# A stack of eight blocks in one kernel: zero rows, plane loads, and shared experts beside a front, reordered

## The chip, the cores and the metric

The kernel runs on one core of one Trainium2 chip. The metric is the device time of one execution in microseconds. All arithmetic here is f32, apart from some bf16 tables of ones and zeros.

## The reference, cut to what matters

The input is 4096 tokens of 256 values. Eight blocks are added to it one after another:

```python
x = x + _L0_attn_a_ref(_layernorm(x), ...)   # mamba: conv, scan over 4 x 1024 steps, 512 channels, 16 states
x = x + _L0_ffn_ref(_layernorm(x), ...)      # 8 experts, top 2, capacity-limited
x = x + _L0_attn_b_ref(_layernorm(x), ...)   # RWKV
x = x + _L0_ffn_ref(_layernorm(x), ...)
x = x + _L1_attn_a_ref(_layernorm(x), ...)   # ssm scan, 256 channels, 16 states; 4 experts, top 2; rms norm with norm_w
x = x + _L1_ffn_ref(_layernorm(x), ...)
x = x + _L1_attn_b_ref(_layernorm(x), ...)   # attention, 16 heads
x = x + _L1_ffn_ref(_layernorm(x), ...)

# _L1_ffn_ref, used twice:
shared = silu(xf @ Sg) * (xf @ Su) @ Sd      # for every token
topk_p, topk_i = top_k(softmax(xf @ Wr), 2)  # 16 experts
y = silu(xf @ wg) * (xf @ wu) @ wd           # each expert, summed with its weights c
return routed + shared
```

## The kernel before, in words

The tokens stand in SBUF as `residual` (`K.X`), 32 tiles of 128 tokens, worked on in eight chunks of four tiles (512 tokens). Stages follow each other. Each engine (V is DVE, S is ACT, G is POOL, T is PE, Q is SP) has its own order of instructions, written out by hand; events (semaphores) tie them together. Each of SP's transfers is issued in the order written, and a wait there holds what stands behind it.

**Scans.** `Scan` (lines 272 on) runs mamba and ssm: a unit is one state of one chunk. SP broadcasts the unit's rows of B and C to all partitions (512 KB, `s_bc`, line 350), into a ring of six buffers. POOL multiplies (line 434), three units ahead; ACT makes the decays, DVE scans, PE sums. `Scan.program` also runs sides beside the units, cut into pieces by ticks: `front(c)` makes the inputs of a chunk, `early(c)` adds up its incoming residual. In the prologue `front(0)` and `early(1)` advance tick by tick together. In the mamba scan SP puts one zero transfer behind every fourth unit (`sync_zero_rows`, line 98): five of 1032 KB to the rows sorted by expert, then eight of 1024 KB to the two planes of results, which later experts fill by token.

**Planes.** A token has two expert results, one in each plane of `results_by_token`. `Planes.sync_tile` (line 1021) loads one tile of both planes, 128 KB each, so eight transfers per chunk. RWKV, the ssm stage and the first stage of sixteen experts take their incoming results so. In the ssm stage `PairSum` has ACT make diagonal matrices of the weights (line 1089), PE multiply by them (line 1100) and DVE add to the residual (line 2473); normalisation on ACT (line 2551) and PE's transposes (line 2656) follow.

**The ssm route.** After the scan a route picks two of four experts for each token, and `SlotTable` makes the list of rows to gather, in eight groups: DVE compares (lines 953, 956), ACT (965) and POOL (975) multiply, PE sums (984). `R.vector_tiles` (lines 881 to 893) finds the expert of each tile and the final weights; `table.vector_rows` (991 to 1000) makes the row numbers. `fold` multiplies the down weights by the inner gain on DVE (line 2737). PE waits for it ahead of the first expert tile; POOL's gathers (line 2281) wait for the row numbers.

**Sixteen experts with a shared expert** (`moe1_stage`, twice). The first use begins with what the ssm block owes: `NormedCombine` adds the two planes (DVE, line 1130), squares (ACT, 1140), takes a root (POOL, 1146), scales and adds to the residual (DVE, 1158, 1162). Then normalise (ACT, 2873), transpose (PE, 2942), copy (ACT, 2890), logits (PE, 2948). This is the front of a chunk. After all eight fronts the shared expert runs chunk by chunk on PE: gate and up (line 2959), down (line 2969). Beside it DVE routes and makes the slot table. For the first three chunks (`BESIDE`), during which DVE routes, POOL does the products and the additions to the residual from ACT's copies; later DVE does them. The slot table's groups stand two by two ahead of chunks 3 to 6 on DVE, the tile steps and row numbers ahead of chunk 7. The planes of a chunk are loaded into the buffers of the shared expert's activations, which are free in the front. SP's order there: planes of chunks 0 and 1, router and shared weights, 32 expert weights (line 2824), then planes of chunk 2 and a row store.

## Time and profile before

| what | us |
|---|---|
| median of 3 runs | 5258.45 |
| lowest, highest | 5258.2, 5264.23 |
| profiled execution | 5258.9 |
| its span | 5257.2 |
| PE, DVE, POOL, ACT busy | 4016.0, 2871.3, 2504.2, 2291.7 |
| mamba scan | to about 1040 |
| 8 experts, RWKV, 8 experts | to 2364 |
| ssm scan; route and four-expert tiles | to 2946; to 3400 |
| front of 16 experts; shared expert; expert tiles | to 3521; to 3630; to 3780 |
| attention; second stage of 16 experts with the end | to 4851; to 5257 |

The profile is of one execution, and its stages follow each other on one core, so a share of busy time over the whole span is a mean over stages with different limits. Each place of the change is to be read in its own stage: what ended the last wait there.

### The profile page before, as it was taken

Reading aid. Unit: us, or ns where it says so; the run is one execution under the profiler, and the core shown is the slowest. Engines: PE = TensorE matmul, PEld = TensorE weight load, DVE = VectorE, ACT = ScalarE, POOL = GpSimd, SP = SyncE. Lnnn points to the kernel's source line nnn. Section 1 sums busy time; section 2 is a strip of 40 time slices with the busy share of each in tenths; the row PEclk is TensorE's granted clock in tenths of the full one; section 3 lists DMA queues with packets and bytes.
Section 4 is the critical chain, followed back from the end, with each engine's and each line's share of the span. In section 5 each row is a group of like instructions: output and inputs, shape, how many; then the busy total and the mean of one; then the engine's idle time right before and its main releaser. Section 6 shows DMA issues by size and latency. Waiting matters only on the chain.

```text
span 5257.2 us, 49460 instructions
## 1 busy us (share of the span) xinstructions
PE 4016.0 (76%) x14864; PEld 2274.2 (43%) x14866; DVE 2871.3 (55%) x5621; ACT 2291.7 (44%) x4134; POOL 2504.2 (48%) x2152
## 2 busy tenths in 40 slices
PE   5788888769948778995777699849757677777892
PEld 2333333357715556772333366536522222223671
DVE  5899999841156663115888622264344545455432
ACT  5565666321156663114555233333335444555341
POOL 4899999822222333115778444324542413122355
PEclk8999999969968888997888799959857777788796
DMA  7765555512110001214555311231552222220245
GB/s 154 188 158 140 136 143 145 144 49 101 63 49 23 26 25 59 101 58 132 153 148 144 98 45 46 62 122 52 145 95 39 51 39 44 37 37 20 68 126 131
DMA packets 326109, 472.75 MB, mean 90 GB/s; under 512 B 36458, under 2 KB 182870, under 8 KB 325770
## 3 DMA queue, kind: packets, MB, share of 16 engines
q1 hardware_dynamic: 292416, 389.08, 28.2%
q0 software_dynamic: 29184, 76.12, 5.2%
...
## 4 chain that ended last, share of the span: by engine, by line
PE 36%; DVE 8%; ACT 6%; issue 5%; POOL 5%; DMA 3%; SPq 1%; DVEq 0%; POOLq 0%; ACTq 0%
PE s_gate_up L2303 7%; PE s_result_sum L2319 4%; PE s_hidden_sum L1742 3%; PE s_result_sum L1753 3%; PE s_out_sum L3603 3%; PE s_scores_T L3590 2%; PE s_shared L2959 2%; PE s_scores L3554 2%; DVE s_decay L369 2%; ACT s_weights_T L3409 1%; PE s_shared L2969 1%; POOL s_gathered L1043 1%; POOL s_h L434 1%; PE s_transposed L2293 1%; PE s_mid_transposed L2312 1%
## 5 line engine op out<-in xcount | busy, mean ns | idle before, releaser
L434 POOL TENSOR_TENSOR s_h<-s_dtu,s_bc 128x1024 f32<-128x1024 f32 x384 | 902.7, 2362 | 121.8 <-PE s_y_sum L476 77.8
L476 PE MATMUL s_y_sum<-s_h,identity 128*128 128x512 f32 x1536 | 791.0, 655 | 160.4 <-POOL s_h L443 146.2
L401 ACT ACTIVATE s_decay<-s_dt,s_A 128x512 f32<-128x512 f32 x768 | 498.4, 681 | 339.7 <-DVE s_h L376 333.2
L476 PEld LDWEIGHTS s_y_sum<-s_h,identity 128*128 128x128 f32 x1536 | 302.4, 207 | 611.6 <-issue 321.7
L3409 ACT ACTIVATE s_weights_T<-s_scores_T 128x1024 f32<-128x1024 f32 (+3 forms) x384 | 300.3, 812 | 403.7 <-PE s_scores_T L3590 402.3
L2303 PE MATMUL s_gate_up<-s_w_gate_up,s_rowsT 128*128 x1184 | 419.2, 486 | 2.6 <-issue 2.1
L3473 POOL TENSOR_SCALAR_AFFINE_SELECT s_weights_T<-s_weights_T 128x256 f32<-128x256 f32 x256 | 104.3, 411 | 625.1 <-ACT s_weights_T L3409 623.1
L443 POOL TENSOR_TENSOR s_h<-s_h,s_bc 128x512 f32<-128x512 f32 x256 | 326.3, 1275 | 43.6 <-DVE s_h L369 26.5
L2362 DVE TENSOR_TENSOR s_mid<-s_act,s_gate_up 128x128 f32<-128x128 f32 (+1 forms) x228 | 92.7, 407 | 454.8 <-ACT s_act L2335 454.8
L369 DVE TENSOR_TENSOR_SCAN s_decay<-s_decay,s_h 128x512 f32<-128x512 f32 x256 | 307.6, 1217 | 53.4 <-POOL s_h L434 26.3
L369 DVE TENSOR_TENSOR_SCAN s_decay<-s_decay,s_carry,s_h 128x512 f32<-128x512 f32 x256 | 322.4, 1275 | 23.7 <-ACT s_decay L401 10.3
L376 DVE TENSOR_TENSOR s_h<-s_decay,s_bc 128x512 f32<-128x512 f32 x512 | 331.1, 666 | 0.0
L2281 POOL DMA_INDIRECT s_rows<-rows_by_token,s_rows_at x228 | 235.4, 1032 | 163.4 <-issue 92.7
...
L1742 PE MATMUL s_hidden_sum<-s_rowsT,s_w_inter 128*128 128x320 f32 x1024 | 282.0, 437 | 0.9 <-ACT s_rowsT L1677 0.9
L1753 PE MATMUL s_result_sum<-s_w_exp_out,s_hidden 128*128 128x256 f32 x1280 | 279.1, 379 | 1.1 <-issue 1.1
L3554 PE MATMUL s_scores<-s_keys,s_queries 96*128 96x512 bf16 (+3 forms) x550 | 194.3, 393 | 101.0 <-DVE s_maxima L3254 27.9
L3251 DVE CUSTOM_DVE_ANT_0 s_scores<-s_scores,s_mask_add 128x256 f32<-128x256 f32 (+2 forms) x380 | 189.2, 509 | 134.3 <-PE s_scores L3554 125.1
L2303 PEld LDWEIGHTS s_gate_up<-s_w_gate_up,s_rowsT 128*128 128x128 f32 x1184 | 209.6, 192 | 116.0 <-issue 105.6
L1686 ACT ACTIVATE s_hidden<-s_hidden_sum 128x320 f32<-128x320 f32 x128 | 56.0, 437 | 467.3 <-PE s_hidden_sum L1742 467.3
L3590 PE MATMUL s_scores_T<-s_queries,s_keys 99*128 99x512 bf16 (+3 forms) x768 | 218.0, 373 | 53.1 <-DMA s_queries<-parts_of_max 32.8
L1753 PEld LDWEIGHTS s_result_sum<-s_w_exp_out,s_hidden 128*128 128x128 f32 x1280 | 241.9, 190 | 34.3 <-issue 2.1
...
## 6 DMA issues: line engine op xcount, KB each, us to landing
s_bc<-s_bc_rows SPq DMA_DIRECT2D x384, 512.0 KB, 5.4
sorted_results<-s_result SPq DMA_DIRECT2D x160, 128.0 KB, 2.3
s_w_inter<-in_L_ffn_experts_inter SPq DMA_DIRECT2D x16, 1024.0 KB, 5.1
s_w_exp_out<-in_L_ffn_experts_out SPq DMA_DIRECT2D x16, 1024.0 KB, 8.2
...
results_by_token<-zeros SPq DMA_DIRECT2D x8, 1024.0 KB, 8.0
...
```

The source lines that it names most:

```text
L369: V.e.tensor_tensor_scan(decay if d < k else self.h[r][:, d, :], decay, self.h[r][:, d, :], self.carry[:, i, d:d + 1] if c % CPB else 0.0, ...
L376: V.e.tensor_tensor(self.h[r][:, d, :], self.decay[:, (2 * g + d) % 4, :], self.bc[r][:, 1, :], ALU.mult).then_inc(*(self.weighed_v if d = ...
L401: S.e.activation(self.decay[:, (2 * g + d) % 4, :], dt[q // self.passes % 2][:, at, :], ACT.Exp, scale=A[:, at, g % ns:g % ns + 1]).then_i ...
L434: G.e.tensor_tensor(self.h[r][:], dtu[q // self.passes % 2][:, at:at + 2, :], mid(self.bc[r][:, 0, :], 2), ALU.mult).then_inc(*self.fed.up())
L443: G.e.tensor_tensor(h, h, self.bc[g % self.RING][:, 1, :], ALU.mult).then_inc(*self.weighed_g.up())
L476: made = T.e.matmul(self.y[:, d, :], ident[:], self.h[r][:, d, :], start=False, stop=g % ns == ns - 1)
L1742: made = T.e.matmul(hb[half][:, 0:HALF], w_in[r][:, k, i * P:(i + 1) * P], xsT[r][:, k, half * HALF:(half + 1) * HALF], start=k == 0, stop ...
L1753: made = T.e.matmul(ob[n % 2][:, 0:D], hT[:, i, t * P:(t + 1) * P], w_out[r][:, i, :], start=i == 0, stop=i == KI - 1)
L2303: made = T.e.matmul(self.gb[j % 2][:, at:at + n], self.xT[j % 2][:, k, :], self.gu_flat[:, bass.ds(expert[j] * (DT * 2 * F) + (k * 2 * F + ...
L3409: S.e.activation(PT[n % 2][:, 2 * pair:2 * pair + 2, o:CH], st[pair][:, :, o:CH], ACT.Exp, scale=HD ** -0.5).then_inc(*weighed.up())
L3554: T.e.matmul(f[:, 0:n_keys], QS[u % 2][0:ROWS, h, qt * P:(qt + 1) * P], KS[u % 2][0:ROWS, h, half * CH:half * CH + n_keys], start=True, st ...
L3590: made = T.e.matmul(st[pair][:, i, o:CH], KS[u % 2][:, h, kt * P:(kt + 1) * P], QS[u % 2][:, h, qh * CH + o:(qh + 1) * CH], start=True, st ...
```

## The change

Five parts. (1) The zeros go out in transfers of half the size, planes first, one behind every eighth unit. (2) The planes of a chunk come in two transfers of 512 KB. (3) In the ssm prologue `early(1)` runs 24 ticks behind `front(0)`. (4) In the ssm route the fold goes from DVE to ACT, and the tile steps go behind the row numbers. (5) In the first stage of sixteen experts three chunks of the shared expert stand in the front, two beside the route, and the slot table comes after chunk 4; SP issues four weights per chunk behind that chunk's planes.

```diff
@@ sync_zero_rows
-        for to, n, half in ((self.sorted_in, CAPPED_SLOTS // P, D // 2 + 1), (self.planes, 2 * NT, D // 2)):
-            for s0 in range(0, n, 8):
-                Q.e.dma_start(to[s0 * P:(s0 + 8) * P, :].rearrange("(p a) (b c) -> p (a b) c", p=P, b=2),
-                              mid(self.zeros[:, 0:half], 16)).then_inc(*self.zeroed.dma())
+        for to, n, width in ((self.planes, 2 * NT, D), (self.sorted_in, CAPPED_SLOTS // P, D + 2)):
+            for s0 in range(0, n, 4):
+                Q.e.dma_start(to[s0 * P:(s0 + 4) * P, :].rearrange("(p a) c -> p a c", p=P),
+                              mid(self.zeros[:, 0:width], 4)).then_inc(*self.zeroed.dma())
@@ Scan.program
-            second.until(tick)
+            second.until(tick - self.behind)
@@ mamba_stage
-        sc.sync(rows_made, rows[32:64, :], lambda g: steps(zeros, 1 if g % 4 == 3 else 0))
+        sc.sync(rows_made, rows[32:64, :], lambda g: steps(zeros, 1 if g % 8 == 7 else 0))
@@ Planes
+    def sync_half(self, c, i):
+        self.K.Q.e.dma_start(self.to(c)[i], self.from_dram[i][:, chunk_tiles(c), :]).then_inc(*self.arrived[c % 2].dma())
+    def sync(self, c):
+        self.sync_half(c, 0)
+        self.sync_half(c, 1)
@@ ssm stage
-    sc = Scan(K, M, 1, NS, (1, 2), prologue=32)
+    sc = Scan(K, M, 1, NS, (1, 2), prologue=32, behind=24)
-            c, i = divmod(g, NS)
-            if c + 3 < NC and i % 2 == 0 and i < 2 * TPC:
-                pieces(c + 3, range(i // 2, i // 2 + 1))
+            c, n = divmod(g, NS)
+            if c + 3 < NC and n in (2, 6):
+                pairs.sync_half(c + 3, n // 4)
...
     def fold():
-        V.wait_ge(*weights_here.now())
-        flat = w_d[:].rearrange("p e k c -> p (e k) c")
-        V.e.tensor_tensor(flat, flat, last(gain[:].rearrange("p e k -> p (e k)"), D), ALU.mult).then_inc(*folded.up())
+        S.wait_ge(*weights_here.now())
+        for e in range(E):
+            for k in range(F // P):
+                made = S.e.activation(w_d[:, e, k, :], w_d[:, e, k, :], ACT.Copy, scale=gain[:, e, k:k + 1])
+        made.then_inc(*folded.up())
...
-        if g == 2:
-            R.vector_tiles()
     table.vector_rows()
-    fold()
+    R.vector_tiles()
@@ moe1_stage
-    BESIDE = 3
+    early = K.owed == "normed"
+    BESIDE, EARLY = (5, 3) if early else (3, 0)
-        owed = NormedCombine(K, MS, xn, norm_w, hs + hm)
-    copies = MS.sb("shared_copies", [P, 2, CH])
+        owed = NormedCombine(K, MS, xn, norm_w, [R.work[:, 2 * i:2 * i + 2, :] for i in range(4)])
+    copies = [MS.sb(f"shared_copies{i}", [P, 2, CH]) for i in range(2 if early else 1)]
+    FRONTS = in_order("f0 f1 f2 f3 f4 f5 f6 f7")
+    ORDER = in_order("f0 f1 i0 f2 f3 o0 i1 f4 f5 o1 i2 f6 f7 o2") if early else FRONTS
+    GPSIMD_ORDER = in_order("f0 f1 f2 f3 i0 f4 f5 o0 i1 f6 f7 o1 i2 o2") if early else FRONTS
...
         for c in range(NC):
             if owed is not None and c + 2 < NC:
                 owed.sync_chunk(c + 2)
+            for e in range(c * E // NC, (c + 1) * E // NC):
+                for j, n in enumerate(("Wg", "Wu")):
+                    Q.e.dma_start(w_gu[:, e, :, j * F:(j + 1) * F],
+                                  W["L1_ffn_" + n][e].rearrange("(k p) f -> p k f", p=P)).then_inc(*experts_here.dma())
             Q.wait_ge(*ln.used.at(c))
...
+        for kind, c in ORDER:
+            {"f": front, "i": shared_in, "o": shared_out}[kind](c)
+        for c in range(EARLY, max(NC, LAST)):
+            if c < NC:
+                shared_in(c)
+                shared_out(c)
+            if c == EARLY:
+                R.tensor_rank()
             for g in groups(c):
                 table.tensor_group(g)
```

`f` is a front, `i` the gate and up part of a shared chunk (`shared_in`), `o` its down part (`shared_out`); ACT and PE follow `ORDER`, POOL `GPSIMD_ORDER`. DVE keeps its fronts, route, groups in that order; with `LAST` now 9, its groups stand ahead of chunks 5, 6, 7 and behind chunk 7.

On PE, in the ssm prologue (`s_pair_0`, `s_pair_1` are a chunk's planes), before, from the middle of chunk 1's eight pair products, behind which chunk 0's transposes stand:

```order
L1100 MATMUL s_front<-s_pair_0,s_pair_weights 128x256
L1100 MATMUL s_front<-s_pair_1,s_pair_weights 128x256
L2656 MATMUL s_front<-identity,s_xn 128x128 x8
L2662 MATMUL s_front<-s_xT,s_w_bc 32x512 x2
L2670 MATMUL s_front<-s_xT,s_w_delta 128x512 x2
L2671 MATMUL s_front<-s_ones_row,s_b_delta 128x512
L2670 MATMUL s_front<-s_xT,s_w_delta 128x512 x2
L2671 MATMUL s_front<-s_ones_row,s_b_delta 128x512
L2678 MATMUL s_front<-identity,s_stat 1x128 x3
```

and now, from chunk 0's last two products:

```order
L1104 MATMUL s_front<-s_pair_0,s_pair_weights 128x256
L1104 MATMUL s_front<-s_pair_1,s_pair_weights 128x256
L2657 MATMUL s_front<-identity,s_xn 128x128 x8
L2663 MATMUL s_front<-s_xT,s_w_bc 32x512 x2
L2671 MATMUL s_front<-s_xT,s_w_delta 128x512 x2
L2672 MATMUL s_front<-s_ones_row,s_b_delta 128x512
L2671 MATMUL s_front<-s_xT,s_w_delta 128x512 x2
L2672 MATMUL s_front<-s_ones_row,s_b_delta 128x512
L2679 MATMUL s_front<-identity,s_stat 1x128 x3
L1104 MATMUL s_front<-s_pair_0,s_pair_weights 128x256
L1104 MATMUL s_front<-s_pair_1,s_pair_weights 128x256
```

The transposes (line 2657 now) stand directly behind chunk 0's eight products; chunk 1's stand behind the bound's products (line 2679).

On PE, in the first stage of sixteen experts, before (the last two fronts, then the shared chunks):

```order
L2942 MATMUL s_shared<-identity,s_y_rows 128x128 x8
L2948 MATMUL s_logits<-s_w_router,s_xT 128x16 x8
L2942 MATMUL s_shared<-identity,s_y_rows 128x128 x8
L2948 MATMUL s_logits<-s_w_router,s_xT 128x16 x8
L2959 MATMUL s_shared<-s_xT,s_w_shared_gate_up 128x512 x8
L2969 MATMUL s_shared<-s_w_shared_down,s_shared_mid 128x256 x8
L820 MATMUL s_rank_within_tile<-s_mask,before 128x512
L820 MATMUL s_tile_totals<-s_mask,ones_bf 128x512
L2959 MATMUL s_shared<-s_xT,s_w_shared_gate_up 128x512 x8
L2969 MATMUL s_shared<-s_w_shared_down,s_shared_mid 128x256 x8
L2959 MATMUL s_shared<-s_xT,s_w_shared_gate_up 128x512 x8
L2969 MATMUL s_shared<-s_w_shared_down,s_shared_mid 128x256 x8
```

and now, from the first front on:

```order
L2975 MATMUL s_shared<-identity,s_y_rows 128x128 x8
L2981 MATMUL s_logits<-s_w_router,s_xT 128x16 x8
L2975 MATMUL s_shared<-identity,s_y_rows 128x128 x8
L2981 MATMUL s_logits<-s_w_router,s_xT 128x16 x8
L2991 MATMUL s_shared<-s_xT,s_w_shared_gate_up 128x512 x8
L2975 MATMUL s_shared<-identity,s_y_rows 128x128 x8
L2981 MATMUL s_logits<-s_w_router,s_xT 128x16 x8
L2975 MATMUL s_shared<-identity,s_y_rows 128x128 x8
L2981 MATMUL s_logits<-s_w_router,s_xT 128x16 x8
L3003 MATMUL s_shared<-s_w_shared_down,s_shared_mid 128x256 x8
L2991 MATMUL s_shared<-s_xT,s_w_shared_gate_up 128x512 x8
L2975 MATMUL s_shared<-identity,s_y_rows 128x128 x8
```

A gate and up piece (line 2991) stands behind each pair of fronts, a down piece (line 3003) behind the next pair.

On DVE, at the end of the ssm route, before (tile steps between the third and fourth group):

```order
L881 TENSOR_TENSOR s_tile_compare<-iota,s_end_tile 128x320
L882 TENSOR_REDUCE s_tile_expert_f<-s_tile_compare 128x80
L883 TENSOR_SCALAR s_tile_expert_f<-s_tile_expert_f 128x80
L884 CAST s_tile_expert<-s_tile_expert_f 128x80
L886 CAST pick_row<-s_slots 128x32 x2
L889 TENSOR_TENSOR s_route_red<-pick_weight 128x32
L890 TENSOR_SCALAR s_route_red<-s_route_red 128x32
L891 RECIPROCAL s_route_red<-s_route_red 128x32
L893 TENSOR_TENSOR pick_weight<-pick_weight,s_route_red 128x32 x2
L894 ISA
L953 TENSOR_TENSOR s_one_hots<-iota,s_tile_of 128x640
```

and now, behind the last group:

```order
L957 TENSOR_TENSOR s_one_hots<-iota,s_lane_of 128x1024
L992 TENSOR_SCALAR s_row_of_place<-s_result_sum 128x80
L997 TENSOR_TENSOR s_row_of_place<-s_row_of_place,s_result_sum 128x80
L1006 TENSOR_SCALAR s_empty_place<-s_row_of_place 128x80
L1008 SCALAR_TENSOR_TENSOR s_results_at<-s_row_of_place,s_empty_place 128x80
L1001 TENSOR_SCALAR s_rows_at<-s_results_at 128x80
L882 TENSOR_TENSOR s_tile_compare<-iota,s_end_tile 128x320
L883 TENSOR_REDUCE s_tile_expert_f<-s_tile_compare 128x80
L884 TENSOR_SCALAR s_tile_expert_f<-s_tile_expert_f 128x80
L885 CAST s_tile_expert<-s_tile_expert_f 128x80
```

The tile steps (line 882 on) stand behind the row numbers (line 1001), and no fold follows on DVE.

## Rows read from the trace of the kernel before

**Rows 1.** Windows of the mamba scan: busy time of POOL's products (line 434).

```profile
core 0: us, POOL busy (x), PEclk, DMA share, GB/s
51.00:160.00 109.00, 51.75 (x23) 0.79 0.90 166
160.00:280.00 120.00, 71.29 (x31) 0.92 0.76 201
280.00:960.00 680.00, 435.37 (x186) 0.93 0.55 143
```

**Rows 2.** DMA issues between 50 and 160 us: KB each, median us to landing.

```profile
s_bc<-s_bc_rows SPq DMA_DIRECT2D x23, 512.0 KB, 10.4
sorted_rows<-zeros SPq DMA_DIRECT2D x5, 1032.0 KB, 14.9
results_by_token<-zeros SPq DMA_DIRECT2D x1, 1024.0 KB, 7.7
```

**Rows 3.** Waits between 51 and 160 us: us in total, times, longest.

```profile
POOL s_h L434 <- DMA s_bc<-s_bc_rows: 20.1, 5, 7.1
```

**Rows 4.** Timeline at the start of the ssm stage: start, us, engine, line.

```profile
2374.67 0.23 ACT L2538 ACTIVATE s_A<-s_A 128x32 f32<-128x32 f32 x1 [31.76 <-DMA s_norm_w<-in_L_norm_w]
...
2389.93 2.07 ACT L2551 ACTIVATE s_xn<-residual,s_rn_addend,s_rn_factor 128x256 f32<-128x256 f32 x4 [12.11 <-POOL s_rn_addend L243]
...
2399.65 1.22 DVE L2473 TENSOR_TENSOR residual<-residual,s_front 128x1024 f32<-128x1024 f32 x1 [11.88 <-PE s_front L1100]
2400.91 1.40 DVE L220 BATCH_NORM_STATS2 s_rn_stats<-residual 128x6 f32<-128x256 f32 x4
...
2401.02 1.06 PE L2656 MATMUL s_front<-identity,s_xn 128*128 128x128 f32 x8 [1.41 <-DVE residual L2473]
```

**Rows 5.** Timeline of the ssm route and its first gather.

```profile
2967.52 1.54 DVE L881 TENSOR_TENSOR s_tile_compare<-iota,s_end_tile 128x320 bf16<-128x320 f32 x1
...
2971.88 0.83 DVE L953 TENSOR_TENSOR s_one_hots<-iota,s_tile_of 128x640 bf16<-128x640 f32 x1
...
2984.46 0.83 ACT L965 ACTIVATE s_one_hots<-s_one_hots,s_own_lane 128x640 bf16<-128x640 bf16 x1 [2.10 <-DVE s_one_hots L953]
...
2989.14 0.20 DVE L1000 TENSOR_SCALAR s_rows_at<-s_results_at 128x80 int32<-128x80 int32 x1
2989.26 4.42 DVE L2737 TENSOR_TENSOR s_w_down<-s_w_down,s_inner_gain 128x4096 f32<-128x4096 f32 x1
2990.23 4.51 POOL L2281 DMA_INDIRECT s_rows<-rows_by_token,s_rows_at  x1 [3.56 <-DVE s_rows_at L1000]
...
2996.74 0.66 PE L2293 MATMUL s_transposed<-identity,s_rows 128*128 128x128 f32 x2 [8.70 <-DMA s_rows<-rows_by_token,s_rows_at]
```

**Rows 6.** Window of the first front of sixteen experts, all engines.

```profile
3400.00:3520.00 120.00, 41.55 (x185) 38.38 (x186) 64.25 (x176) 41.76 (x113) 25.13 (x41) 0.50 0.54 164
```

**Rows 7.** SP's queue in that front: the second sixteen weight transfers.

```profile
3420.21 8.15 SPq L2824 DMA_DIRECT2D s_w_gate_up<-in_L_ffn_Wu  x16
```

**Rows 8.** DVE's timeline in that front: the wait for chunk 2's planes.

```profile
3442.43 3.38 DVE L1130 SCALAR_TENSOR_TENSOR s_y_rows<-s_shared_act,pick_weight,s_y_rows 128x256 f32<-128x256 f32 x8 [19.45 <-DMA s_shared_act<-results_by_token]
```

**Rows 9.** PE's timeline from that front to the end of the shared expert.

```profile
3463.92 3.60 PE L2948 MATMUL s_logits<-s_w_router,s_xT 128*128 128x16 f32 x16 [2.18 <-ACT s_xT L2890]
...
3505.40 3.60 PE L2948 MATMUL s_logits<-s_w_router,s_xT 128*128 128x16 f32 x16 [3.13 <-ACT s_xT L2890]
...
3518.07 3.59 PE L2948 MATMUL s_logits<-s_w_router,s_xT 128*128 128x16 f32 x16 [0.69 <-ACT s_xT L2890]
3521.51 9.97 PE L2959 MATMUL s_shared<-s_xT,s_w_shared_gate_up 128*128 128x512 f32 x16
...
3539.47 7.03 PE L2959 MATMUL s_shared<-s_xT,s_w_shared_gate_up 128*128 128x512 f32 x16
...
3566.63 7.03 PE L2959 MATMUL s_shared<-s_xT,s_w_shared_gate_up 128*128 128x512 f32 x16
...
3617.18 7.07 PE L2959 MATMUL s_shared<-s_xT,s_w_shared_gate_up 128*128 128x512 f32 x16
3625.20 3.69 PE L2969 MATMUL s_shared<-s_w_shared_down,s_shared_mid 128*128 128x256 f32 x16 [0.94 <-DVE s_shared_mid L2861]
```

109 lines of the change are left out of this document (57 added, 52 removed).

## The prediction, made before the result was known

> **What bounds the kernel now.** I read the page first, then the stages as windows, then in each stage the waits, and last the timelines around every wait that the change touches. One engine after another sets the pace on this core, so the change is costed stage by stage: mamba scan, RWKV start, ssm start, ssm route, first front of the sixteen experts with its shared expert.
>
> In the mamba scan POOL's products run back to back once the zeros are stored: 680 us for 186 units, 3.66 us each, at a DMA share of 0.55. While the zeros go out, 23 units take 109 us at a share of 0.90 and 31 take 120 at 0.76 [rows 1]. At 3.66 a unit these 54 would take 197.6, so 31.4 us are lost: 24.8 in the first window and 6.6 in the second. The reader is to see that POOL waits for the broadcast of B and C itself, 20.1 us in five waits, which the later windows don't have [rows 3], and that a zero transfer of sorted rows (pieces of 516 B) lands after 14.9 us while one of the result planes (pieces of 512 B) takes 7.7, and that a broadcast beside them takes 10.4 [rows 2].
>
> At the start of the ssm stage PE's transposes of chunk 0 start at 2401.02, though their input is ready at 2392.00 (2389.93 + 2.07): in PE's order the pair sum of chunk 1 stands before them, and its bank is free only when DVE has added it [rows 4]. In the ssm route the chain ends in DVE's table rows, then the first gather, whose issue takes 4.51 us beside DVE's 4.42 us fold, and PE starts at 2996.74 [rows 5].
>
> In the front of the sixteen experts PE is at 1.2 GHz for all 120 us and busy for a third of them [rows 6]. DVE stands 19.45 us for a pair of planes that is queued on SP behind 32 weight transfers, the last 16 of which take 8.15 us to issue [rows 7, 8]. Then comes the shared expert, a PE chain of eight chunks that ends the stage [rows 9].
>
> **The zeros.** Bytes and SP issues: 13 transfers become 26 of half the size, spread over 207 units in place of 51. From the shares, one broadcast costs 0.55 x 3.66 = 2.0 us of all DMA engines. The first window holds 0.90 x 109 - 23 x 2.0 = 52 us of zeros, five of sorted rows and one of planes; the second 0.76 x 120 - 31 x 2.0 = 29 us for seven of planes, so 4.1 each, and 9.6 each for sorted rows. Halved blocks: 2.1 and 4.8 us, now one per 29 us. The DMA engines are then never full. The lowest loss is nothing. The highest that the nearest rows give is by size: a plane block of 4.1 us lost 0.9 each (6.6 over seven), so sixteen at 0.5 and ten sorted blocks at 1.1 lose 19. I take the middle, **10, so 21 us gained** (bounds 12 and 31), since the ring holds three units of lead against a block shorter than one and a half. Pieces of 1,032 B may be cheaper than 516 B ones; no row shows a size above 512 B with an odd end, and I give nothing for it. The Trainium skill ("DMA: Bandwidth & Descriptors", Specifications) says that pieces of 512 B or more run at line rate, by which 516 B pieces should cost what 512 B pieces do; by that rule the halving saves only queueing. The rows above disagree with it, by more than twofold.
>
> **The planes in two transfers per chunk in place of eight.** SP issues six fewer, some 0.46 us each. Bytes are the same. At the RWKV start the first pair comes up to 2.7 us earlier, of which I take 1; at the first front 0.5; elsewhere other work hides them.
>
> **ssm start.** Constants follow the first pair on SP, and ACT waits for the last of them until 2374.67 [rows 4]: 2.3 earlier. Transposes of chunk 0 can follow their normalisation: 9.0 earlier. Against it: PE comes to them colder (I take 3.5, bounds 0 and 9, the length of the doubled PE work); DVE's add and statistics of chunk 1 (1.22 + 1.40 + 0.38 = 3.0) now stand in scan unit 1, where DVE is near its limit; 1.0 for ACT's weights and POOL's factors there. Sum **+4** (bounds -2 and +8).
>
> **ssm route.** The tile steps of 4.36 us (2967.52 to 2971.88) leave the chain and stand behind the row numbers. The row numbers are then ready at 2985.0. The fold leaves DVE; sixteen ACT steps of 128x256, 0.52 us each by the four normalising steps of that size (2.07 [rows 4]), take 8.3 us from 2980.9 on (2984.46 + 0.83 less 4.36 [rows 5]), so end at 2989.2, before the first gathered rows. The first gather needs 1.0 to issue in place of 4.51 and some 2 to land: PE starts near 2990.2 in place of 2996.74: **+6.5** (bounds 3, if the moved tile steps now lengthen the gather as the fold did, and 7.9, both terms in full).
>
> **First front with three shared chunks inside.** SP now issues pairs ahead of weights, so 16 of the 19.45 us go and the logits of chunk 1 end at 3451.3, not 3467.5 (3463.92 + 3.60 [rows 9]). Then PE runs shared-in of chunk 0, 9.97 at the low clock as measured, to 3461.3. Two rounds follow of two fronts, an out and an in. Two fronts took 20.7 where a transfer held them (3463.92 to 3505.40, halved) and 12.7 at the end (3505.40 to 3518.07). Now ACT serves both fronts and shared work in strict order, so I take 20.3. Out plus in takes 10.7 at full clock (7.07 + 3.69 less overlap [rows 9]), 21.3 at half; I take 14.1 as the clock climbs. Two rounds are 68.8, the last two fronts 12.7 and 1.6 for ACT's turn: logits end at 3544.4, **22.7 later** than 3521.66. Behind them stand one out and five chunks: 5.4 for the out with its wait, 27.2 for the two chunks beside the route (3539.47 to 3566.63), 3 x 12.6 (3566.63 to 3617.18 is four), 2 for DVE's last add: 72.4, where from 3521.7 to that add before (3625.20 + 3.69 + 0.7) it was 107.9. Then what used to be covered: groups 6 and 7 of the slot table with the row numbers, 6.9 (five took 17.3, from 2971.88 to 2989.14 [rows 5]), and the tile steps, 4.4, less some 2 in which they fill DVE's idle time: 9.3; and 0.9 from the row numbers to the gather (2989.34 to 2990.23 [rows 5]). First gather at 3627.0; before, by the same 0.9 behind the last add, at 3630.5. Of these 3.5 I take **+2.5**, one off for the loads on POOL and ACT that no row shows beside the new order (bounds -17, everything shared at the low clock, and +28). What was 108 us of well packed PE is now packed into a front that has other limits, so most of what leaves the tail returns in the front.
>
> The second such stage keeps its order; its SP order changes, but nothing waits there for pairs: nothing.
>
> **Sum.** 21 + 1 + 4 + 6.5 + 0.5 + 2.5 = 35.5 us off the profiled execution's 5258.9, 5223.4. The median of the runs is 5258.45, so the two stand 0.45 apart, which I leave alone.
>
> **Rivals.**
> 1. *Fast front.* DVE's chain lets the fronts run at 12.7 a pair, and shared work lifts PE to 2.4 GHz early: 2 x 7.6 + 2 x 3.4 + 3 for the first shared-in at full clock = 25 more: 5198. For it: the tail of the front before did 12.7. Against: ACT's order couples fronts to PE's shared results.
> 2. *Low clock.* Each shared piece stands between waits and stays at 1.2 GHz, as PE did all through this front [rows 6]: 14 for two rounds, 5 for the first chunks behind: 5242. The Trainium skill ("TensorE: Matmul & The Clock Gate", HAM oscillation) describes bursts between waits that start cold each time. By that rule the trace agrees: 0.50 for 120 us [rows 6], and the first shared-in takes 9.97 against 7.07 later.
> 3. *Zeros still cost.* The upper loss of 19: 5232.
> 4. *Zeros don't gain.* If transfer time alone counted, all 81 us of it stay and the loss stays 31.4: 5244. That is the skill's rule above taken at its word.
> 5. *Slower.* On the queue each zero block stands between two broadcasts. If a broadcast is held for the block's whole time and POOL with it, 16 x 2.1 + 10 x 4.8 = 82 us are lost in place of 31.4: 5295. It makes the kernel slower once more than 56 of the 82 are exposed (31.4 + 14.5 of other gains + 10.5). Before, 31.4 of 81 were, with full engines. Unlikely.
>
> **Chances.** Forecast 0.45, rival 1 0.18, rival 2 0.15, rival 3 0.12, rival 4 0.03, rival 5 0.04, something else 0.03. The range goes from rival 1 to rivals 2 and 4, 5198 to 5244. This kernel can be told from no change at 0.2%, 10.5 us. Only rivals 2 to 4 together come within that (0.06); slower 0.04; faster 0.90.
>
> **What would show it.** Right: in the mamba scan no long POOL wait for a broadcast, and units 23 to 54 at 3.7 us; PE's transposes of chunk 0 right behind ACT's normalisation; a first ssm gather of 1.0 us; no 19 us DVE stall, the last logits some 22 us later, the first gather of the sixteen experts about 2 to 3 us earlier. Wrong: a granted clock of 0.50 through the interleaved front, POOL waits at every eighth scan unit, or DVE as the last to end before the first gather by more than 10 us.

## The result, and the profile after

The changed kernel takes 5221.05 us (median of 4 runs, 5211.93 to 5230.75), the kernel before 5258.32 (4 runs, 5254.15 to 5264.23). The ratio is 0.9929, 95% interval 0.9908 to 0.9949. The forecast was 5223, so the total came as forecast, to within 2 us. The terms behind it did not all do so, and that is what the rest is about.

The profiled execution of the changed kernel is the longest of its four: 5230.75 us, span 5229.0, against a span of 5257.2 before. Cut at the first instruction of each stage in the two traces (SP's first transfer, or PE's first expert product; the front of sixteen experts is cut from its rest at DVE's first step of the route, and the rest ends at POOL's first gather), the 28.2 us between the spans fall like this. The medians lie 37.3 us apart, so the table accounts for an execution that gained less than the median one.

| stretch, from first instruction to first instruction | before | changed | difference | forecast |
|---|---|---|---|---|
| mamba scan | 1038.82 | 1004.33 | -34.5 | -21 |
| 8 experts, to RWKV | 406.95 | 406.93 | 0.0 | 0 |
| RWKV | 600.20 | 607.53 | +7.3 | -1 |
| 8 experts | 319.00 | 320.39 | +1.4 | 0 |
| ssm stage | 582.14 | 583.95 | +1.8 | -4 |
| route, to the first expert product | 49.63 | 43.59 | -6.0 | -6.5 |
| four-expert tiles | 405.59 | 406.69 | +1.1 | 0 |
| front of 16 experts | 119.37 | 135.64 | +16.3 | +22.2 |
| rest of that stage, to the first gather | 108.83 | 83.97 | -24.9 | -25.2 |
| expert tiles | 145.10 | 146.44 | +1.3 | 0 |
| attention | 1077.13 | 1085.49 | +8.4 | 0 |
| second stage of 16 experts, end | 404.44 | 404.05 | -0.4 | 0 |

**Scan.** POOL's products in the changed kernel in the windows of [rows 1] (columns as there):

```profile
51.00:160.00 109.00, 67.55 (x29) 0.84 0.58 157
160.00:280.00 120.00, 75.11 (x33) 0.92 0.60 158
280.00:960.00 680.00, 440.97 (x188) 0.94 0.60 160
```

62 units by 280 us where there were 54, and in these windows the DMA share is never above 0.60. The issues while the planes' zeros go out (60 to 520 us), and then the sorted rows' (520 to 820 us), to be read beside [rows 2]:

```profile
results_by_token<-zeros SPq DMA_DIRECT2D x16, 512.0 KB, 5.8
```

```profile
s_bc<-s_bc_rows SPq DMA_DIRECT2D x82, 512.0 KB, 4.8
sorted_rows<-zeros SPq DMA_DIRECT2D x10, 516.0 KB, 7.2
```

A broadcast lands after 4.8 us here, and after 4.7 in the window of [rows 2], where it took 10.4 before; a half block of sorted rows lands after 7.2. From 51 us to the end of the scan POOL waited 29.6 us in ten waits for broadcasts in the kernel before ([rows 3] has five of them). In the changed kernel it waits 0.2 us, once.

**ssm start.** PE's timeline, to be read beside [rows 4]:

```profile
2364.10 1.97 PE L2657 MATMUL s_front<-identity,s_xn 128*128 128x128 f32 x8 [7.46 <-ACT s_xn L2552]
...
2371.47 3.78 PE L2671 MATMUL s_front<-s_xT,s_w_delta 128*128 128x512 f32 x4 [0.68 <-ACT s_rows L2568]
...
2377.18 3.78 PE L2671 MATMUL s_front<-s_xT,s_w_delta 128*128 128x512 f32 x4
```

The transposes stand 0.06 us behind the normalisation, as forecast, but each group of delta products takes 3.78 us, where the kernel before took 1.98. The window of all engines (busy of PE, its weight loads, DVE, ACT and POOL, then the granted clock, DMA share and GB/s) has the clock beside it, 0.50, the lower of PE's two levels (1.2 of 2.4 GHz), though PE is busy 10.96 of these 12 us:

```profile
2372.00:2384.00 12.00, 10.96 (x12) 2.84 (x10) 0.13 (x1) 1.00 (x1) 0.00 (x0) 0.50 0.53 137
```

Then, from the timeline of all engines:

```profile
2401.33 0.36 SPq L1022 DMA_DIRECT2D s_pair<-results_by_token  x1
...
2401.73 9.89 SPq L351 DMA_DIRECT2D s_bc<-s_bc_rows  x4
...
2407.60 2.35 POOL L435 TENSOR_TENSOR s_h<-s_dtu,s_bc 128x1024 f32<-128x1024 f32 x1 [4.27 <-DMA s_bc<-s_bc_rows]
```

SP's first load of chunk 3's planes waits there until PE has summed the pair of chunk 1; broadcasts stand behind it and POOL waits 4.27 us.

**Route.** The rows that answer to [rows 5]:

```profile
2961.85 0.20 DVE L1001 TENSOR_SCALAR s_rows_at<-s_results_at 128x80 int32<-128x80 int32 x1
2961.97 0.48 DVE L882 TENSOR_TENSOR s_tile_compare<-iota,s_end_tile 128x320 bf16<-128x320 f32 x1
...
2962.94 1.20 POOL L2283 DMA_INDIRECT s_rows<-rows_by_token,s_rows_at  x1 [3.56 <-DVE s_rows_at L1001]
...
2966.72 0.66 PE L2295 MATMUL s_transposed<-identity,s_rows 128*128 128x128 f32 x2 [5.97 <-DMA s_rows<-rows_by_token,s_rows_at]
```

The compare of the tile steps takes 0.48 us where it took 1.54 beside a POOL product. The gather is issued in 1.20 us, not 4.51.

**Front of sixteen experts.** DVE's timeline, the stalls only, then PE's, to be read beside [rows 8] and [rows 9], and windows of the front and of the rest (columns as in [rows 6]):

```profile
3405.27 3.38 DVE L1133 SCALAR_TENSOR_TENSOR s_y_rows<-s_route_work,pick_weight,s_y_rows 128x256 f32<-128x256 f32 x8 [4.13 <-DMA s_route_work<-results_by_token]
...
3435.00 0.17 DVE L1158 TENSOR_SCALAR s_y_sums<-s_y_sums 128x4 f32<-128x4 f32 x1 [13.37 <-ACT s_y_squares L1143]
...
3466.71 0.17 DVE L1158 TENSOR_SCALAR s_y_sums<-s_y_sums 128x4 f32<-128x4 f32 x1 [14.55 <-ACT s_y_squares L1143]
...
3509.05 0.69 DVE L836 TENSOR_REDUCE s_route_red<-s_logits 128x32 f32<-128x512 f32 x1 [26.50 <-PE s_logits L2981]
```

```profile
3419.20 3.60 PE L2981 MATMUL s_logits<-s_w_router,s_xT 128*128 128x16 f32 x16 [7.59 <-ACT s_xT L2902]
3422.63 9.69 PE L2991 MATMUL s_shared<-s_xT,s_w_shared_gate_up 128*128 128x512 f32 x16
...
3451.85 5.31 PE L3003 MATMUL s_shared<-s_w_shared_down,s_shared_mid 128*128 128x256 f32 x16
3457.00 7.03 PE L2991 MATMUL s_shared<-s_xT,s_w_shared_gate_up 128*128 128x512 f32 x16
...
3484.51 6.04 PE L3003 MATMUL s_shared<-s_w_shared_down,s_shared_mid 128*128 128x256 f32 x16
3490.39 7.03 PE L2991 MATMUL s_shared<-s_xT,s_w_shared_gate_up 128*128 128x512 f32 x16
...
3505.41 3.59 PE L2981 MATMUL s_logits<-s_w_router,s_xT 128*128 128x16 f32 x16 [0.69 <-ACT s_xT L2902]
...
3514.51 7.03 PE L2991 MATMUL s_shared<-s_xT,s_w_shared_gate_up 128*128 128x512 f32 x16
```

```profile
3373.41:3509.05 135.64, 73.03 (x273) 55.14 (x274) 64.42 (x177) 50.97 (x129) 37.42 (x50) 0.64 0.49 145
3509.05:3593.02 83.97, 65.97 (x241) 40.41 (x242) 61.63 (x77) 20.03 (x30) 30.78 (x18) 0.91 0.01 2
```

The 19.45 us stall is gone, but DVE now stands 13.37 and 14.55 us for squares, which ACT takes behind its turn with a shared chunk.

### The profile page after: what moved, and what is told of

Read it like the earlier page. It is cut to its first block, busy times and chain, and to the rows that moved or that the text cites. A ratio compares the mean times of both kernels' runs of the same rounds, so it can differ in the third digit from the quotient of the medians.

```text
span 5229.0 us, 49359 instructions
## 1 busy us (share of the span) xinstructions
PE 4032.2 (77%) x14864; PEld 2280.5 (44%) x14866; DVE 2867.2 (55%) x5612; ACT 2302.5 (44%) x4158; POOL 2513.9 (48%) x2160
## 4 chain that ended last, share of the span: by engine, by line
PE 38%; DVE 8%; ACT 6%; issue 4%; POOL 4%; DMA 3%; SPq 1%; DVEq 0%; POOLq 0%; another core or an unknown queue 0%; ACTq 0%
PE s_gate_up L2305 7%; PE s_result_sum L2321 4%; PE s_hidden_sum L1745 3%; PE s_result_sum L1756 3%; PE s_out_sum L3641 3%; PE s_scores_T L3628 2%; PE s_shared L2991 2%; PE s_scores L3592 2%; DVE s_decay L370 2%; PE s_shared L3003 1%; ACT s_weights_T L3447 1%; POOL s_gathered L1047 1%; POOL s_h L435 1%; PE s_transposed L2295 1%; DVE s_maxima L3292 1%
## 5 line engine op out<-in xcount | busy, mean ns | idle before, releaser
L477 PE MATMUL s_y_sum<-s_h,identity 128*128 128x512 f32 x1536 | 774.2, 644 | 124.4 <-POOL s_h L444 112.8
L3628 PE MATMUL s_scores_T<-s_queries,s_keys 99*128 99x512 bf16 (+3 forms) x768 | 220.7, 378 | 45.2 <-DMA s_queries<-parts_of_max 33.9
```

What stands on the lines that cost most here:

```text
L477: made = T.e.matmul(self.y[:, d, :], ident[:], self.h[r][:, d, :], start=False, stop=g % ns == ns - 1)
L3628: made = T.e.matmul(st[pair][:, i, o:CH], KS[u % 2][:, h, kt * P:(kt + 1) * P], QS[u % 2][:, h, qh * CH + o:(qh + 1) * CH], start=True, st ...
```

## The experiments

Each stage is closed by a barrier, so several edits can be read in one kernel by the lengths of their stages. The kernel before was run beside each group; its median was 5263.78 (13 runs), 5259.46 (19), 5257.67 (7). Lengths in us from the profile of each, with the median time and the ratio to before:

| kernel | median | ratio (95%) | mamba | RWKV | ssm | route | front + rest | attention |
|---|---|---|---|---|---|---|---|---|
| zeros_only | 5228.13 | 0.9941 (0.9923 to 0.996) | 1001.7 | 607.3 | 583.6 | 49.6 | 118.2 + 105.7 | 1073.0 |
| planes_only | 5251.62 | 0.9981 (0.9971 to 0.999) | 1033.1 | 609.8 | 582.6 | 49.5 | 113.7 + 106.5 | 1073.4 |
| pairs_later | 5216.21 | 0.992 (0.9901 to 0.9939) | 1002.3 | 606.1 | 579.5 | 43.9 | 135.6 + 83.9 | 1078.5 |
| behind_0 | 5222.11 | 0.9926 (0.991 to 0.9943) | 1003.2 | 606.3 | 582.9 | 43.8 | 135.4 + 84.0 | 1078.5 |
| sp_order_only | 5209.84 | 0.9904 (0.9887 to 0.9921) | 1002.3 | 603.8 | 584.8 | 43.4 | 101.8 + 106.4 | 1086.2 |
| order_undone | 5227.33 | 0.9931 (0.991 to 0.9953) | 1003.2 | 607.5 | 584.9 | 44.0 | 114.6 + 106.6 | 1083.2 |
| big_blocks_fold | 5256.24 | 0.9988 (0.9977 to 1.0) | 1029.5 | 610.9 | 583.7 | 46.2 | 119.6 + 107.2 | 1077.0 |
| old_pieces_tiles | 5240.59 | 0.9963 (0.9952 to 0.9975) | 1016.9 | 607.1 | 583.5 | 46.8 | 118.2 + 106.7 | 1076.3 |
| planes_ahead | 5200.31 | 0.9893 (0.9877 to 0.991) | 1006.6 | 605.7 | 580.5 | 43.5 | 90.8 + 106.7 | 1077.1 |
| front_freed | 5201.51 | 0.9892 (0.9875 to 0.9908) | 1007.1 | 605.8 | 579.4 | 43.4 | 115.7 + 83.8 | 1082.5 |
| every_4 | 5227.15 | 0.994 (0.9924 to 0.9957) | 1014.7 | 605.8 | 583.8 | 43.5 | 135.3 + 83.9 | 1078.7 |
| before_again | 5245.11 (1 run) | | 1029.3 | 600.8 | 583.6 | 49.5 | 118.6 + 105.7 | 1074.7 |

### The zeros: zeros_only, big_blocks_fold, old_pieces_tiles, every_4

**zeros_only**: the kernel before with `sync_zero_rows` and its `g % 8 == 7` from the change.

> The kernel before with the zeros of the change alone (half the size, planes first, one behind every eighth unit). Theory A (the loss beside the zeros goes whole, and what the changed kernel lost again in RWKV and attention is the scatter of those stages): the end of the mamba scan comes 33 to 36 us before the 1038.8 us of the kernel before, RWKV takes 598 to 608 us without any tie to the scan, and the total is 25 to 38 us shorter than before. Theory B (half of it is given back later, in RWKV and attention, because of the zeros): mamba 34 us earlier, RWKV 607 us and attention 1085 us again, total 15 to 20 us shorter. The forecast's own term was 21 us with bounds of 12 and 31.

Mamba ends at 1001.7. The three profiles with the old zeros end it at 1038.8, 1029.3 and 1033.1; their mean is 1033.7. The eight kernels with the new zeros end it at 1001.7 to 1007.1, 1003.8 in the mean. So the zeros are worth some 30 us (22 to 37 between single profiles): theory A, not the forecast's 21. The cause is in POOL's waits for broadcasts, which sum to 29.6, 26.2 and 27.0 us in the three profiles with the old zeros and to 0.8 us at most in the eight with the new ones. The total agrees: 0.9941 is 31 us off.

**big_blocks_fold**: in the kernel before

```diff
-        sc.sync(rows_made, rows[32:64, :], lambda g: steps(zeros, 1 if g % 4 == 3 else 0))
+        sc.sync(rows_made, rows[32:64, :], lambda g: steps(zeros, 1 if g % 8 == 7 else 0))
     def fold():
-        V.wait_ge(*weights_here.now())
+        S.wait_ge(*weights_here.now())
...
```

and the sixteen ACT steps of the change called behind the scalar groups.

> The kernel before with two edits in two stages. Zeros: the old 13 transfers of 1 MB, but one behind every eighth unit. Theory A (what counts is that blocks stand too close for the DMA engines to catch up): nearly all of the 31 us goes, mamba ends at 1003 to 1010. Theory B (a single 1 MB block outlasts the ring's lead each time): five sorted blocks still cost 3 to 5 us each, mamba ends at 1018 to 1030. Route: the fold on ACT, tile steps left between the groups. Both theories: first gather issued in 1.0 us, 3.5 us less than the 49.6 from the route's first transfer to the first expert product.

**old_pieces_tiles**: half blocks every eighth unit in the old pieces, and the tile steps moved with the fold left on DVE:

```diff
+        for to, n, half in ((self.planes, 2 * NT, D // 2), (self.sorted_in, CAPPED_SLOTS // P, D // 2 + 1)):
+            for s0 in range(0, n, 4):
+                Q.e.dma_start(to[s0 * P:(s0 + 4) * P, :].rearrange("(p a) (b c) -> p (a b) c", p=P, b=2),
+                              mid(self.zeros[:, 0:half], 8)).then_inc(*self.zeroed.dma())
```

> The kernel before with two edits in two stages. Zeros: half-size blocks, planes first, every eighth unit, but in the old pieces of 512 and 516 B. Theory A (rows: 516 B pieces cost 4.8 us of all DMA engines for half a MB, whatever the spacing): sorted blocks land after about 7 us, as those with 1032 B pieces do, mamba ends at 1002 to 1008. Theory B (piece size matters): sorted blocks of 516 B pieces land later than 8 us, and their DMA share is higher than the changed kernel's 0.63. Route: tile steps behind the row numbers, the fold still on DVE, now behind them: the first gather is issued 4.4 us earlier, but PE waits for the fold, so 2 to 3.5 us less than 49.6.

**every_4**: the changed kernel with `g % 4 == 3` again.

> The changed kernel with the same half-size zero blocks one behind every fourth unit, so the spacing alone goes back. Theory A (halving the block and the whole pieces do it, the ring's lead covers any single block): mamba ends within 5 us of 1004. Theory B (what counts is the bytes per unit of time): DMA share near 0.7 while they go out, mamba ends at 1010 to 1020.

Spaced alone, the 1 MB blocks end mamba at 1029.5, within theory B's range, and POOL's own wait for broadcasts from 51 to 520 us reads

```profile
POOL s_h L434 <- DMA s_bc<-s_bc_rows: 7.3, 4, 4.0
```

That is 7.3 us where 26.2 to 29.6 were waited for at the old spacing, so the scan's end does not follow these waits. What else is in it are two waits of DVE (line 579) for PE's sums at the end of a chunk, 7.01 us to 201.18 and 7.60 us to 446.29; the waits of this kind in the eight kernels with the new zeros are 4.8 at most.

Halved, in old pieces, mamba ends at 1016.9. Halved and in whole pieces, at the 1001.7 to 1007.1 above. The half blocks of the planes in pieces of 512 B and then those of the sorted rows in pieces of 516 B land after

```profile
results_by_token<-zeros SPq DMA_DIRECT2D x16, 512.0 KB, 6.0
```

```profile
sorted_rows<-zeros SPq DMA_DIRECT2D x10, 516.0 KB, 9.0
```

The planes' 6.0 us are what pieces of 1024 B take too (5.8 to 6.0 in the nine kernels that have them), but the sorted rows' 9.0 us stand against 7.2 to 7.9 in pieces of 1032 B, with the same bytes. So theory B was right that they land later than 8 us, though not of the DMA share, which is 0.63 from 520 to 820 us as in the changed kernel. But the late blocks did not hold the broadcasts: POOL waits 1.0 us for them in the whole scan. Of the 15 us over zeros_only 13.7 are two waits of DVE for PE:

```profile
664.76 1.23 DVE L579 TENSOR_TENSOR s_u<-s_y_sum,s_z 128x1024 f32<-128x1024 f32 x1 [6.37 <-PE s_y_sum L476]
...
791.10 1.23 DVE L579 TENSOR_TENSOR s_u<-s_y_sum,s_z 128x1024 f32<-128x1024 f32 x1 [7.31 <-PE s_y_sum L476]
```

Ahead of the second one PE stood at the lower clock (columns as in [rows 6]):

```profile
774.00:790.00 16.00, 13.97 (x16) 4.52 (x15) 9.79 (x11) 11.07 (x18) 14.99 (x8) 0.50 0.55 177
```

Whether the pieces had a part in that, one profile can't say.

Whole pieces at the old spacing (every_4) end mamba at 1014.7, within theory B's 1010 to 1020. Here POOL's waits, small and many, account for the 11 us over the 1003.8; those from 51 to 520 us read

```profile
POOL s_h L435 <- DMA s_bc<-s_bc_rows: 11.6, 11, 1.8
```

big_blocks_fold and old_pieces_tiles also split the route. With the fold alone on ACT it takes 46.2 us, 3.4 off the 49.6 of before; with the tile steps alone moved, 46.8, 2.8 off. The fold's rows in big_blocks_fold, from the timeline of all engines:

```profile
2989.76 6.47 ACT L2738 ACTIVATE s_w_down<-s_w_down,s_inner_gain 128x256 f32<-128x256 f32 x16
...
2994.79 1.19 POOL L2281 DMA_INDIRECT s_rows<-rows_by_token,s_rows_at  x1 [3.56 <-DVE s_rows_at L1000]
...
2997.84 0.66 PE L2293 MATMUL s_transposed<-identity,s_rows 128*128 128x128 f32 x2 [5.23 <-DMA s_rows<-rows_by_token,s_rows_at]
```

Sixteen steps take 6.47 us, 0.40 each, and end before the gathered rows have landed. In old_pieces_tiles, where DVE keeps the fold, the first gather passes it and the third does not:

```profile
2974.21 1.20 POOL L2281 DMA_INDIRECT s_rows<-rows_by_token,s_rows_at  x1 [3.56 <-DVE s_rows_at L1000]
...
2976.70 4.42 DVE L2737 TENSOR_TENSOR s_w_down<-s_w_down,s_inner_gain 128x4096 f32<-128x4096 f32 x1
2977.03 4.97 POOL L2281 DMA_INDIRECT s_rows<-rows_by_token,s_rows_at  x1 [0.30 <-issue]
...
2981.23 0.66 PE L2293 MATMUL s_transposed<-identity,s_rows 128*128 128x128 f32 x2 [9.20 <-DVE s_w_down L2737]
```

PE's transposes there wait 9.20 us, to the fold's end.

Of mamba: the spacing alone doesn't give the gain, and with half blocks in whole pieces the spacing is worth some 11 us, all of it in POOL's waits. What the pieces are worth to the scan is not shown, nor what the block's size is worth by itself: the half blocks go out planes first in every kernel that has them, and repeats of one zero order lie up to 5 us apart with the new zeros and 9.5 with the old.

### Planes and later stages: planes_only, before_again

> The kernel before with two plane transfers of 512 KB per chunk in place of eight of 128 KB. Theory A: nothing but the issues of the first pair in each stage moves; RWKV stays within 4 us of its 600.2, the ssm prologue reaches its first row store 2 us earlier, total within 5 us of before. Theory B: the large transfers cost RWKV its 7 us (607 us instead of 600.2), total 5 to 10 us longer.

> The kernel before once more, for a second profile of its stages. Theory A (a stage scatters by some us from one execution to the next, and the first profile of before had a short RWKV): RWKV 604 to 611 us here, mamba ends at 1032 to 1040. Theory B (the shorter scan or the planes lengthen RWKV): RWKV 600 us again.

**planes_only** is the kernel before with two transfers per chunk. It is 10 us faster (0.9981). Some 5 us of that stand in the front of sixteen experts, 113.7 us where five profiles with eight transfers and the old order read 118.2 to 119.6: SP has twelve issues fewer ahead of chunk 2's planes, and DVE waits for planes 36.3 us there in place of 41.9. The forecast gave 0.5 for that. No stage shows the rest. In RWKV its first chunk is 0.7 to 1.1 us shorter, as forecast. But RWKV as a whole is not settled: the two profiles of the kernel before have 600.2 and 600.8, the changed kernel and its eleven relatives 603.8 to 610.9, three of them (zeros_only, big_blocks_fold, old_pieces_tiles) with not one instruction of RWKV changed. So it is not the planes alone. It may be the scatter of single profiles, though the two of one kernel lie only 0.6 apart. Attention is alike: 1073.0 to 1077.1 in the six profiles of kernels built on the one before, 1077.1 to 1086.2 in the eight built on the changed one, where it has the same instructions. Its windows, before and then changed (columns as in [rows 6]), show which engine took longer over them:

```profile
3775.63:4852.76 1077.13, 749.79 (x3732) 283.12 (x3732) 525.73 (x1591) 498.19 (x648) 327.87 (x424) 0.77 0.24 46
```

```profile
3739.46:4824.95 1085.49, 762.42 (x3732) 287.66 (x3732) 530.68 (x1591) 498.81 (x648) 328.44 (x424) 0.76 0.24 46
```

The same 3732 products keep PE busy 12.6 us longer, at a slightly lower mean clock; ACT and POOL take the same time to within 1 us. So the 8.4 us of attention go with PE's clock. In RWKV it is less plain: PE is busy 7.6 us longer in the changed kernel (434.2 for 426.6), but only 2.1 longer in zeros_only, whose RWKV is as long. What sets the clock stays open; no run here isolates it.

### ssm start: pairs_later, behind_0

```diff
-            if c + 3 < NC and n in (2, 6):
-                pairs.sync_half(c + 3, n // 4)
+            if c + 3 < NC and n in (6, 10):
+                pairs.sync_half(c + 3, n // 8)
```

> The changed kernel with the planes of chunk c+3 issued behind scan units 6 and 10 in place of 2 and 6. Theory A: in the changed kernel SP stands at the planes of chunk 3, which wait until PE has added the pair of chunk 1, now 24 ticks later, and the broadcasts of units 3 on are queued behind (POOL waits 4.3 us). Then the time from POOL's first product to the second row store of the ssm scan goes from 43.6 us back to about 39, and the ssm stage is 4 to 5 us shorter. Theory B: the 43.6 us come from DVE's and ACT's work on chunk 1 that now stands in the first units, and the time stays within 1 us.

SP no longer stands there: seven broadcasts go out ahead of the load.

```profile
2368.56 30.76 SPq L351 DMA_DIRECT2D s_bc<-s_bc_rows  x7
2399.36 0.47 SPq L1022 DMA_DIRECT2D s_pair<-results_by_token  x1
```

From POOL's first product to the second row store it is 42.6 us, not 39 (43.6 in the changed kernel): 1.0 of the 4.7 us over the kernel before was SP's wait, the rest stands beside chunk 1's add, statistics and pair products in the first units. (The kernel before has 38.9 us there in the profile of the forecast and 39.8 in before_again, so the excess may be a microsecond less.) So theory B is right of the interval. Yet the stage is 4.5 us shorter, 3.5 of it before the first product, in the same PE work:

```profile
2366.94 3.78 PE L2671 MATMUL s_front<-s_xT,s_w_delta 128*128 128x512 f32 x4 [0.68 <-ACT s_rows L2568]
...
2371.94 1.98 PE L2671 MATMUL s_front<-s_xT,s_w_delta 128*128 128x512 f32 x4
```

The second group of delta products runs at 2.4 GHz there. This is hardly an accident of one execution: pairs_later, planes_ahead and front_freed, which share the edit, have 1.98 us and 579.4 to 580.5 for the stage; the changed kernel, sp_order_only, order_undone and every_4 have 3.78 and 583.8 to 584.9.

> The changed kernel with chunk 1's pair sum back beside chunk 0's front (behind=0). Theory A: the shift by 24 ticks gains 8.5 us to the first row store and gives all back (5.5 us at PE's low clock, 4.7 us behind SP's wait), so the ssm stage without it is 1 to 3 us shorter than the 583.9 us of the changed kernel. Theory B (the forecast): the shift is worth 2 to 4 us, and without it the stage is that much longer.

**behind_0** (`behind=0` in the changed kernel) has 582.9: theory A. The shift alone costs 1.1 us; with the loads put off it gains 3.4.

### Front of sixteen experts: sp_order_only, order_undone, planes_ahead, front_freed

**sp_order_only** sets `early = False` in the changed kernel: engines in the old order, SP in the new one. **order_undone** takes the whole stage from the kernel before, with its planes in two transfers.

> The changed kernel with the first stage of sixteen experts back in the old engine order (all fronts, then eight shared chunks, three beside the route, table early), but with SP's new order (planes ahead of weights). Stage from its first planes to its first gather: 228.2 us before, 219.6 in the changed kernel. Theory A (SP's order and not the three shared chunks in the front carries the gain): the front takes 100 to 105 us (the 19.45 us stall goes), the tail stays at 106 to 109, so 206 to 214 in all, and this kernel beats the changed one by 5 to 13 us. Theory B (the forecast's working, where the fronts are held by transfers and turns either way): the front loses only 5 to 8 of its 119 us, stage 218 to 222.

> The changed kernel with the whole first stage of sixteen experts as before, SP's order too (planes in two transfers). Theory A: it reads like the kernel before with two plane transfers per chunk alone, 220 to 224 us for the stage, so the reorder is worth only 1 to 4 us of the 8.6 between the two profiles. Theory B: 228 us, the reorder is worth 8 us.

```profile
3367.75:3469.51 101.76, 43.24 (x193) 40.07 (x194) 64.26 (x176) 41.77 (x113) 24.90 (x40) 0.50 0.65 194
```

Theory A, clearly: with SP's order alone the front is 101.8 us and the stage 208.2, where three shared chunks inside make it 219.6, and the old order altogether 221.2. SP's order is worth 13.0 us, and the interleaving gives 11.4 of them back. (With SP's order goes the move of the incoming planes to other buffers, `R.work` in the diff; the two were not run apart.) The total follows: 5209.84. The interleaving lengthens the front by 33.9 us and shortens the rest by 22.5. Of the 33.9, 28.0 are DVE's waits for squares, which sum to 30.3 us in the changed kernel's front and to 2.3 in this one.

What DVE still waits for in it are planes, at every second chunk:

```profile
3399.03 3.38 DVE L1133 SCALAR_TENSOR_TENSOR s_y_rows<-s_route_work,pick_weight,s_y_rows 128x256 f32<-128x256 f32 x8 [3.55 <-DMA s_route_work<-results_by_token]
...
3419.01 3.38 DVE L1133 SCALAR_TENSOR_TENSOR s_y_rows<-s_route_work,pick_weight,s_y_rows 128x256 f32<-128x256 f32 x8 [3.58 <-DMA s_route_work<-results_by_token]
...
3438.92 3.38 DVE L1133 SCALAR_TENSOR_TENSOR s_y_rows<-s_route_work,pick_weight,s_y_rows 128x256 f32<-128x256 f32 x8 [3.50 <-DMA s_route_work<-results_by_token]
```

**planes_ahead** takes these away, with the old engine order and pairs_later:

```diff
+        if owed is not None:
+            owed.sync_chunk(2)
         for c in range(NC):
-            if owed is not None and c + 2 < NC:
-                owed.sync_chunk(c + 2)
...
+            if owed is not None and c + 3 < NC:
+                owed.sync_chunk(c + 3)
             Q.wait_ge(*ln.used.at(c))
```

> Meant as the best version: the changed kernel with all fronts ahead of the shared chunks again (as in the run of SP's order alone), the ssm pair loads behind units 6 and 10, and in the first stage of sixteen experts the planes of chunk c+3 issued ahead of the wait for chunk c's normalisation, where they stood behind it. Theory A (three stalls of 3.5 us of DVE at every second chunk are SP standing in that wait): they go, the front falls from 101.8 to 90 to 93 us, the ssm stage from 584.8 to about 580, total 12 to 17 us under SP's order alone, near 5195. Theory B (the planes would come no earlier, since buffers or bandwidth hold them): front stays above 100, total 4 to 5 us under, near 5205.

DVE's waits for planes, then windows of front and rest:

```profile
DVE s_y_rows L1133 <- DMA s_route_work<-results_by_token: 13.6, 1, 13.6
```

```profile
3368.77:3459.55 90.78, 43.25 (x193) 40.07 (x194) 63.98 (x177) 41.41 (x113) 27.40 (x40) 0.50 0.71 217
3459.55:3566.28 106.73, 93.42 (x322) 54.18 (x322) 64.87 (x85) 24.58 (x38) 31.71 (x21) 0.96 0.00 1
```

The front is 90.8 us: of the waits for planes only the stage's first is left. Theory A of the front; the total, 5200.31, is 9.5 under sp_order_only, less than the 12 to 17 expected. Between the two profiles, which lie 18.5 apart, the stage gives 10.7 (208.2 to 197.5) and the ssm stage 4.4. The others are not edited: attention is 9.1 shorter, the mamba scan 4.3 and RWKV 1.9 longer.

**front_freed** keeps the interleaving but lets DVE and POOL run ahead:

```diff
...
+    SCALAR_ORDER = in_order("f0 f1 s4 i0 f2 f3 s6 o0 i1 f4 f5 o1 i2 f6 f7 o2") if early else FRONTS
-    GPSIMD_ORDER = in_order("f0 f1 f2 f3 i0 f4 f5 o0 i1 f6 f7 o1 i2 o2") if early else FRONTS
+    GPSIMD_ORDER = in_order("f0 f1 f2 f3 f4 i0 f5 f6 o0 i1 f7 o1 i2 o2") if early else FRONTS
...
```

(`s4` is the squares of chunk 4; SP as in planes_ahead, in the ssm stage too.)

> The changed kernel (three shared chunks inside the front) with the ssm pair loads behind units 6 and 10, planes of chunk c+3 ahead of the wait, and the squares of chunks 4 and 6 taken by ACT ahead of its shared piece, POOL's root and factors of chunks 4, 6 ahead of its products. Theory A (the front is long because DVE stands 13.4 and 14.6 us for squares behind ACT's shared piece, which waits for PE): the front falls from 135.6 to 112 to 120 us, the stage to 196 to 205. Theory B (each round is held by PE's shared pieces and ACT's turns, and DVE's wait is slack): front stays at 130 to 136.

```profile
3368.67:3484.39 115.72, 70.14 (x273) 52.74 (x274) 65.58 (x176) 50.65 (x129) 39.22 (x50) 0.66 0.56 170
3484.39:3568.16 83.77, 66.01 (x242) 40.47 (x242) 61.43 (x77) 20.04 (x30) 30.95 (x18) 0.91 0.00 1
```

Theory A: 115.7 us for the front, 19.9 less, and 199.5 for the stage. Two edits share this, and DVE's waits part them: those for squares fall by 13.0 us, from 30.3 to 17.3, and those for planes by 4.7, from 18.4 to 13.7. So the waits behind ACT's turn were the greater part of what the interleaving cost, and 17.3 us of them are left. Its total, 5201.51, can't be told from planes_ahead. Both beat the changed kernel by some 20 us.

## Why the prediction was right, and where its parts were not

- **Zeros, 21 forecast, some 30 measured.** The step that failed is the residual of 10 us, taken as the middle between nothing and 19. With blocks halved, spaced and in whole pieces POOL's wait for broadcasts is 0.2 us: the loss doesn't shrink with the block's size, it ends. The lower bound, nothing, was right. The upper one was no bound: by the forecast's own rows the first window lost 24.8 us to five sorted blocks and one of planes, 4.8 a sorted block where the forecast took 2.2. The forecast also said that later windows have no wait for broadcasts; from 160 to 280 us there were five, 9.5 us in all. The sign that it named came: units 23 to 54 went at 3.7 us each. The rule that pieces of 512 B or more run at line rate (Trainium skill, "DMA: Bandwidth & Descriptors", Specifications), by which I had rival 4, is not borne out for pieces of 516 B: half a block in pieces of 516 and of 1032 B, both above it, lands after 9.0 and 7.2 us. For 512 against 1024 B it agrees (6.0 and 5.8 us).
- **Planes.** 1.5 us forecast in all, 0.5 of it at the first front. There planes_only gained 5.
- **ssm, 4 gained by the forecast, 1.8 lost as measured.** The transposes came 11.1 us earlier, by 2.3 + 9.0 as worked out. Chunk 1's work in the first units cost 4.7 where 4.0 was taken (one of it SP's wait, which I had missed: in SP's order the load of chunk 3 waits for the pair sum that was put off). The step that failed is the cold PE, 3.5: the products to the softplus cost 2.6 + 5.5 = 8.1 us more, near the upper bound of 9. Four more profiles of the old ssm stage (before_again, zeros_only, big_blocks_fold, old_pieces_tiles) have 583.5 to 583.7 us where the first had 582.1, so the loss may be nearer nothing.
- **Route, -6.5 forecast, -6.0 measured.** The fold on ACT takes 0.40 us a step where I took 0.52, hidden either way. Its two parts alone sum to 6.2. The moved tile steps give 2.8 of their 4.36 alone, where PE waits for the fold. The gather's issue is 1.20, not 1.0, and its rows land 2.58 us behind it, where some 2 were taken.
- **Front with shared chunks, +22.2 and -25.2 forecast, +16.3 and -24.9 measured.** Each place was where the working had it: first shared piece 49.2 us after the stage began (49.0 forecast), rounds of 31.7 and 33.4 us (34.4 taken), 11.6 for the last two fronts (14.3 taken), rest 83.97 (83.6). The pair of fronts at 20.3 was right (19.7 and 20.6), and the reason given, ACT in strict order, is the one that front_freed shows. The clock was at 0.64 of full in the mean, above rival 2 and below rival 1. What the forecast did not ask is what SP's order would have done alone: it put the lost stall and the interleaving into one sum, +2.5 net, and the runs show 13.0 and -11.4. The stage as a whole went from 228.2 us (224.3 in before_again) to 219.6; with the old order (order_undone) it is 221.2, so most of what it gained came from the planes' two transfers, and 1.6 from the order.
- **What nothing in the forecast covers:** attention is 8.4 us longer with its instructions unchanged, and RWKV 7.3 longer where 1 less was forecast. With the ssm stage's 5.8, the route's 0.5 and 3.4 in the other stages these are 26.4 us, against 13.5 that mamba and 5.6 that the front with its rest gave beyond the forecast. So the profiled execution gained 7.3 us less than forecast, and the median one 1.8 more: the profiled one is 9.7 us above the median. That the total fell within 2 us of the forecast is partly luck; with attention and RWKV at their old lengths the profiled execution would have been near 5215, 8 us under the forecast.

Rival 5 (a zero block holds the next broadcast) shows in part in big_blocks_fold, where POOL still waits 7.3 us in four waits beside 1 MB blocks. Beside half a MB at every eighth unit it does not, and at every fourth unit it does again, 11.6 us in eleven waits.
